# Aligned register loads, earlier scatters of the last tiles and an earlier row table in a routed-expert kernel

## The chip, the cores and the metric

The kernel runs on one core of one Trainium2 chip. The metric is device time in microseconds (us) of one launch. The time before is 1503.49 us, the median of three runs (1494.99 to 1507.39).

## The reference

Two layers act on x, 4 sequences of 512 tokens with 512 features (2048 tokens). Layer 0 is a decayed scan over a context of 1024 tokens with two projections, then a gated feed-forward of width 2048 with Hadamard transforms. Layer 1 is an attention over the same context, then a routed feed-forward: 32 experts, the best 8 for each token. The change concerns that last part alone:

```python
router_logits = x2d @ gate_kernel                      # 2048 tokens x 32 experts
routing_weights = jax.nn.softmax(router_logits, axis=-1)
routing_weights, selected_experts = jax.lax.top_k(routing_weights, TOP_K)
routing_weights = routing_weights / jnp.sum(routing_weights, axis=-1, keepdims=True)
w0 = jax.lax.ragged_dot(sorted_inputs, gate_proj, group_sizes, ...)
w1 = jax.lax.ragged_dot(sorted_inputs, up_proj, group_sizes, ...)
inter = jax.nn.silu(w0) * w1
expert_out = jax.lax.ragged_dot(inter, down_proj, group_sizes, ...)
output = jnp.einsum('BKE,BK->BE', per_token, routing_weights)
```

The output is x plus this sum.

## The kernel before, in words

**Sorting.** The 2048 tokens are 16 tiles of 128 rows. For each tile VectorE computes eight places (POS), one for each chosen expert, and GpSimd writes the tile's rows into the DRAM tensor `rows_by_expert` with eight indirect DMAs (`scatter_rows`, L572 to L578), one for each column of POS. Column w of the last three tiles (13, 14 and 15) counts up the semaphore `s_add[w]`; all other scatters count up `s_ids`. The order written out at the end is: tile 13 all eight columns, tile 14 columns 0 to 3, tile 15 columns 0 to 3, and then columns 4 to 7, each for tile 14 and tile 15 (L589 to L594). SyncE meanwhile writes, one after another, a block of padding rows behind each expert's rows (`pad_expert`).

**Tables.** Each expert's rows are padded to whole tiles of 128, so that up to 159 expert tiles (NTILE) are worked off. How many tiles an expert has is known only at run time. PE and VectorE therefore compute (L1555 to L1593) a table TAB of 5 rows of 168 int32 entries (TABLE), in one partition of the buffer EX: row 0 the expert of a tile, row 1 how many pads and expert weights must have landed before it (`due`), row 2 where its weights lie, row 3 its first row in `rows_by_expert`, row 4 the tile where its expert begins. When all is written, `s_tab` is set to 1.

**Where TAB lies.** EX is cut up by a helper `ex(n)` that hands out n float32 entries after the last ones: TCMP 84 entries, CE 1, CI 2, CH 1, TWK 672, and then TAB. So TAB begins at entry 760 of EX, and its rows follow at distances of 168. In both kernels EX itself begins at byte 207232 of a partition, a multiple of 64.

**The expert loop.** All engines run a loop of 19 rounds (LOOPS) of 8 tiles (U), and then 7 tiles (REST). At the start of each round every engine loads what it needs from TAB into its registers with one instruction for each table row (TENSOR_LOAD in the profile). The helpers are `load_ints` (the load is L104) and `load_counts` (the load is L112, and then L114 raises each value to a least one):

- PE: row 2, 12 entries from it\*8 (L104).
- VectorE: row 0, 8 entries from it\*8 (L104).
- ScalarE: row 3, 12 entries from it\*8 + 4 (L104), then row 1, 12 entries from it\*8 + 2 (L112).
- GpSimd: row 4, 8 entries from it\*8 (L112).

Per tile PE transposes the gathered rows of tile t+2 (L1964), waits for VectorE's product of tile t, transposes it (L1981, L1982), multiplies tile t+1 by its expert's gate and up weights (L1702 to L1704, 384 columns), waits for the hidden activations of tile t, split into a high part by ScalarE (`hidden_hi`, L842) and a low part by VectorE (`hidden_lo`, L1603), and multiplies them by the down weights (L1702 to L1704, L1992, L1993, 512 columns). ScalarE's round is written as: the two register loads, then for each tile `hidden_hi`, `tile_hi` (L834), the DMA that gathers a later tile (`load_tile`, L856), and `tile_silu` (L838). GpSimd adds each finished tile to the output with an indirect DMA (L605).

**The first tiles.** ScalarE waits for the scatters of the last tiles' column 0 (`s_add[0]`) and gathers tile 0. It then waits for `s_tab`, loads the first six entries of rows 1 and 3 with one register load (L864), gathers tiles 1 to 3, works on tile 0 and gathers tiles 4 and 5. Tile t waits for column t's scatters too.

```python
act.wait_ge(s_add[0], LANDED)
load_tile(0, 0, 0, 16)
act.wait_ge(s_tab, 1)
act.reg_load(entries, TAB[0:1, 1:4:2, 0:LEAD])
...
with act.Fori(0, LOOPS) as it:
    rows, due = rows_at("tile_row", it * U + 4, U + 4), experts_due("tile_due", it * U + 2, U + 4)
```

Of the kernel before, what the change touches and what calls it, by code (L numbers as in the profile page):

```python
# [22 lines left out]
P = 128  # L23
# [15 lines left out]
TABLE = NTILE + 9  # L39
# [86 lines left out]
def build(nc, a_x, a_ctxT, a_ctxr, a_kv, a_mask, a_winT, a_woutT, a_cols, a_rows, a_wug, a_wdT,  # L126
          a_gk, a_exp, a_ident, a_had, a_hadf, a_tri, d_exp, d_kv, d_row, d_down, a_out):
    ctx = ExitStack()
    with ctx:
# [3 lines left out]
        def sem(name):  # L133
            return ctx.enter_context(nc.semaphore(name))
# [152 lines left out]
        TCMP = ex(TABLE // 2, F16)  # L287
        CE = ex(1)
        CI = ex(2, I32)
        CH = ex(1, F16)  # L290
        TWK = ex(4 * TABLE, p=1).rearrange("p (a t) -> p a t", a=4)

        TAB = ex(5 * TABLE, I32, p=1).rearrange("p (a t) -> p a t", a=5)
# [57 lines left out]
        s_tp, s_tq, s_tab = sem("table_product"), sem("table_step"), sem("tables_ready")  # L351
# [11 lines left out]
        def _(sp):  # L363
# [151 lines left out]
            sp.wait_ge(s_tpad, 2)  # L515
            for e in range(2 * WP):
                pad_expert(e, 16 * e)
            sp.wait_ge(s_tab, 1)

            def replace_expert(e, h):  # L520
                wait_apart(sp, s_wl, e * 16, s_spassed)
# [16 lines left out]
        def _(pool):  # L538
# [59 lines left out]
            pool.sem_inc(s_y, V)

# [18 lines left out]
        def _(act):  # L618
# [226 lines left out]
                return load_ints(act, name, TAB[0:1, 3, bass.ds(t, count)], 0, NE * CAP + (SPARES - 1) * P)  # L845

            def experts_due(name, t, count):
                return load_counts(act, name, TAB[0:1, 1, bass.ds(t, count)], 16, 16 * NE)

            def load_tile(u, used, row, pads):  # L850

# [8 lines left out]
            act.wait_ge(s_add[0], LANDED)  # L860
            load_tile(0, 0, 0, 16)
            act.wait_ge(s_tab, 1)
            entries = [act.alloc_register(f"first{i}") for i in range(2 * LEAD)]
            act.reg_load(entries, TAB[0:1, 1:4:2, 0:LEAD])  # L864
            rows = [act.snap(x, donate=True, min_val=0, max_val=NE * CAP + (SPARES - 1) * P) for x in entries[LEAD:]]
            due = [act.alloc_register(f"first_due{i}") for i in range(LEAD)]
            for to, of in zip(due, entries):
                act.reg_alu(to, of, 16, ALU.max)
                act.free_register(of)
            due = [act.snap(x, donate=True, min_val=16, max_val=16 * NE) for x in due]  # L870
            act.wait_ge(s_spare, 16)
# [35 lines left out]
        def _(dve):  # L907
# [651 lines left out]
            v.tensor_scalar(CI[0:NE, 1:2], CI[0:NE, 0:1], 7, None, ALU.logical_shift_right).then_inc(s_tq, 1)  # L1559
            dve.wait_ge(s_tq, 2)  # L1560
            v.tensor_copy(CH[0:NE, 0:1], CI[0:NE, 1:2]).then_inc(s_tq, 1)
            dve.wait_ge(s_tp, 2)
            v.tensor_copy(CE[0:NE, 0:1], PS[0:NE, 1, 0:1]).then_inc(s_tq, 1)
            v.tensor_copy(CH[0:NE, 1:2], PS[0:NE, 1, 0:1]).then_inc(s_tq, 1)
            dve.wait_ge(s_tq, 4)
            v.tensor_scalar(TCMP[0:NE, :], TROW[0:NE, :], CE[0:NE, 0:1], None, ALU.is_ge).then_inc(s_tq, 1)
            dve.wait_ge(s_tp, 3)
            erow, start = PS[0:1, 2, 0:TABLE], PS[0:1, 2, TABLE:2 * TABLE]
            trow = TROW[0:1, :]
            v.tensor_scalar(TAB[:, 0, :], erow, NE - 1.0, None, ALU.min).then_inc(s_tq, 1)  # L1570
            v.tensor_scalar(TAB[:, 1, :], erow, NE - 1.0, 1.0, ALU.min, ALU.add).then_inc(s_tq, 1)
            v.scalar_tensor_tensor(TWK[:, 0, :], erow, float(LIST), trow, ALU.mult, ALU.add).then_inc(s_tq, 1)
            v.scalar_tensor_tensor(TWK[:, 2, :], trow, 1.0 - SPARES, start, ALU.add, ALU.subtract).then_inc(s_tq, 1)
            v.tensor_scalar(TCUM[:, :], PS[0:1, 2, 2 * TABLE:2 * TABLE + NE], 1.0, None, ALU.add).then_inc(s_tq, 1)
            dve.wait_ge(s_tq, 10)
            v.tensor_scalar(TAB[:, 2, :], TAB[:, 0, :], WP - 1, None, ALU.bitwise_and).then_inc(s_tq, 1)
            v.tensor_scalar(TAB[:, 1, :], TAB[:, 1, :], 16, None, ALU.mult).then_inc(s_tq, 1)
            v.tensor_tensor(TWK[:, 1, :], TWK[:, 0, :], start, ALU.subtract).then_inc(s_tq, 1)

            v.scalar_tensor_tensor(TWK[:, 3, :], erow, float(NE), TWK[:, 2, :], ALU.is_ge, ALU.mult).then_inc(s_tq, 1)  # L1580
            dve.wait_ge(s_tq, 15)
            v.tensor_scalar(TAB[:, 2, :], TAB[:, 2, :], E16, None, ALU.mult).then_inc(s_tq, 1)
# [3 lines left out]
            dve.wait_ge(s_tq, 19)
            v.tensor_scalar(TODD[:, :], TODD[:, :], SPARES - 1, None, ALU.bitwise_and).then_inc(s_tq, 1)
            dve.wait_ge(s_tq, 20)
            v.tensor_tensor(TAB[:, 3, :], TAB[:, 3, :], TODD[:, :], ALU.add).then_inc(s_tq, 1)
# [53 lines left out]
        def _(pe):  # L1643
# [310 lines left out]
            pe.wait_ge(s_tq, 6)  # L1954
# [135 lines left out]
```

## Time and profile before

| | us |
|---|---|
| median of three runs | 1503.49 |
| the three runs | 1494.99, 1507.39, 1503.49 |
| the profiled execution, its own time | 1494.65 |
| its span, first to last instruction | 1492.9 |

The profile is one execution. Engines are PE (matmul), PEld (weight load), DVE (VectorE), ACT (ScalarE), POOL (GpSimd) and SP (SyncE). A q behind an engine (ACTq) marks what its instruction queue does itself, as a register load, without the engine's arithmetic being busy. "x19" counts instructions, "idle before <-" names what ended an engine's wait. In the chain of waits "issue" is time in which the engine waited for nothing that the profile shows.

### The profile page before, as it was taken

The page shows a single profiled execution, that of the slowest core. Times are in us where ns is not written, and L with a number is a line of the kernel's source. Part 1 is how long each engine was busy: PE and PEld are TensorE (multiplying, and loading weights), DVE is VectorE, ACT ScalarE, POOL GpSimd, SP SyncE. Part 2 cuts the span into 40 slices and gives each one's busy share as a digit, 9 for nine tenths or more (in the row PEclk, how much of TensorE's full clock was granted, in tenths as well). Part 3 has the DMA queues.
Part 4 walks back from the last instruction along what each step waited for, and adds up shares of the span by engine and source line. Part 5 has one row for each costly group of instructions (what it writes and reads, how often), then busy time and mean ns, then how long its engine had stood idle before and what let it go on. Part 6 is the DMA issues. An engine that isn't in the chain of part 4 may idle for free.

```text
span 1492.9 us, 27045 instructions
## 1 busy us (share of the span) xinstructions
PE 1384.7 (93%) x7525; PEld 756.2 (51%) x7526; DVE 1021.5 (68%) x2467; ACT 505.9 (34%) x916; POOL 383.3 (26%) x313
## 2 busy tenths in 40 slices
PE   4899999999999999999998499999999998998997
PEld 2344444444444444455554265555665655565554
DVE  7879857976985656788877366666665655565664
ACT  0445543434444434422222123223332322232222
POOL 1000000000000000036667433433433444333343
PEclk9899999999999999999999699999999999999998
DMA  9976776766667787648769888888988888888785
GB/s 370 379 267 211 254 250 219 248 196 211 232 221 222 236 280 261 232 167 303 284 235 353 270 218 222 199 225 228 243 223 217 217 207 211 175 194 204 130 146 84
DMA packets 132696, 345.04 MB, mean 231 GB/s; under 512 B 15008, under 2 KB 19616, under 8 KB 125728
## 3 DMA queue, kind: packets, MB, share of 16 engines
q1 hardware_dynamic: 73488, 206.72, 41.1%
q0 software_dynamic: 34640, 85.74, 26.0%
q10 hardware_dynamic: 24512, 51.89, 11.0%
q8 instruction: 27, 0.44, 0.1%
q14 instruction: 29, 0.24, 0.1%
HBM read 192.68 MB, written 151.62 MB: 231 GB/s over the span
## 4 chain that ended last, share of the span: by engine, by line
PE 66%; DVE 13%; DMA 6%; ACTq 5%; issue 4%; ACT 3%; SPq 1%; DVEq 0%; POOLq 0%
PE PS L1702 17%; PE PS L1704 17%; PE PS L1703 17%; PE PS L1964 4%; ACTq L112 4%; DMA CST<-in_kv 2%; PE PS L1993 2%; PE PS L1992 2%; DMA split_experts<-HT 2%; DMA rows_by_expert<-X 1%; ACTq L104 1%; PE PS L1981 1%; PE PS L1982 1%; DVE HT L1148 1%; DMA X<-in_x 1%
## 5 line engine op out<-in xcount | busy, mean ns | idle before, releaser
L605 POOL DMA_INDIRECT out<-BIG,EX x159 | 247.1, 1554 | 396.6 <-issue 208.6
L1702 PE MATMUL PS<-BIG 128*128 (+1 forms) x795 | 269.5, 339 | 43.9 <-DVE BIG L1603 42.3
L1704 PE MATMUL PS<-BIG 128*128 (+1 forms) x795 | 269.5, 339 | 0.0
L1703 PE MATMUL PS<-BIG 128*128 (+1 forms) x795 | 269.4, 339 | 0.0
L1702 PE MATMUL PS<-HT,BIG 128*128 128x512 f16 (+1 forms) x512 | 194.1, 379 | 3.2 <-DVE HT L1132 1.4
L1703 PE MATMUL PS<-HT,BIG 128*128 128x512 f16 (+1 forms) x512 | 194.1, 379 | 0.0
L1704 PE MATMUL PS<-HT,BIG 128*128 128x512 f16 (+1 forms) x512 | 194.0, 379 | 0.0
L842 ACT ACTIVATE BIG<-PS 128x256 f16<-128x256 f32 x159 | 60.9, 383 | 298.4 <-PE PS L1982 209.1
L577 POOL DMA_INDIRECT rows_by_expert<-HT,POS x128 | 124.8, 975 | 99.5 <-DVE POS L1422 64.4
L1703 PE MATMUL PS<-BIG,EX 128*128 128x512 f16 (+1 forms) x376 | 143.2, 381 | 0.0
L1704 PE MATMUL PS<-BIG,EX 128*128 128x512 f16 (+1 forms) x376 | 143.2, 381 | 0.0
L1702 PE MATMUL PS<-BIG,EX 128*128 128x512 f16 (+1 forms) x376 | 143.0, 380 | 0.0
L1603 DVE TENSOR_TENSOR BIG<-PS,BIG 128x256 f16<-128x256 f32 x159 | 67.4, 424 | 94.8 <-ACT BIG L842 93.7
L1607 DVE SCALAR_TENSOR_TENSOR BIG<-PS,BIG 128x192 f32<-128x192 f32 x159 | 56.6, 356 | 100.3 <-ACT BIG L838 100.3
L1702 PEld LDWEIGHTS PS<-BIG 128*128 128x128 f16 x795 | 78.1, 98 | 92.4 <-issue 52.9
L1598 DVE SCALAR_TENSOR_TENSOR BIG<-PS,BIG 128x512 f16<-128x512 f32 x159 | 109.9, 691 | 15.8 <-ACT BIG L834 5.7
L1616 DVE TENSOR_SCALAR BIG<-PS,BIG 128x512 f32<-128x512 f32 x159 | 119.3, 751 | 0.0
L668 ACT ACTIVATE HT<-HT 128x1280 f16<-128x1280 f32 x64 | 81.2, 1268 | 95.2 <-DMA split_experts<-HT 93.9
L1964 PE MATMUL PS<-ident,BIG 128*128 128x128 f32 x636 | 98.7, 279 | 11.8 <-DMA BIG<-rows_by_expert 10.1
L569 POOL MEMSET HT<- 128x105 f32 x1 | 0.2, 185 | 422.6 <-DMA split_experts<-HT 422.6
L1704 PEld LDWEIGHTS PS<-BIG 128*128 128x128 f16 x795 | 78.3, 98 | 58.7 <-issue 1.4
L838 ACT ACTIVATE BIG<-PS 128x192 f32<-128x192 f32 x159 | 52.5, 330 | 153.4 <-PE PS L1704 153.4
(264 smaller groups left out, 2254.5 us busy)
## 6 DMA issues: line engine op xcount, KB each, us to landing
BIG<-rows_by_expert ACTq DMA_DIRECT2D x159, 280.0 KB, 4.8
HT<-in_experts SPq DMA_DIRECT2D x64, 640.0 KB, 4.7
BIG<-split_experts SPq DMA_DIRECT2D x32, 1152.0 KB, 8.4
split_experts<-HT SPq DMA_DIRECT2D x96, 320.0 KB, 2.4
CST<-in_kv SPq DMA_DIRECT2D x64, 256.0 KB, 4.8
split_context<-RT SPq DMA_DIRECT2D x64, 256.0 KB, 4.5
BIG<-split_context SPq DMA_DIRECT2D x7, 2048.0 KB, 11.4
rows_by_expert<-X SPq DMA_DIRECT2D x32, 280.0 KB, 7.8
```

What stands on the lines that cost most here:

```text
L112: eng.reg_load(loaded, table)
L577: pool.indirect_dma_start(d_row, bass.IndirectOffsetOnAxis(ap=POS[:, t % ZN, c:c + 1], axis=0), ZR[:, t % ZN, :], None).then_inc(s_ids[t % ...
L605: pool.indirect_dma_start(a_out, bass.IndirectOffsetOnAxis(ap=IDY[:, u % V:u % V + 1], axis=0), yt[u % V], None, compute_op=ALU.add).then_ ...
L668: act.activation(eoh, est[h], ACT.Copy, scale=E_S).then_inc(s_eh, 1)
L842: act.activation(eah[p], PS[:, 4, 0:2 * P], ACT.Copy).then_inc(s_ah2, 1)
L1598: v.scalar_tensor_tensor(xl[p], PS[:, p, :].rearrange("p (k n) -> p k n", n=P), H_S, xh[p], ALU.mult, ALU.subtract).then_inc(s_xl, 1)
L1603: v.tensor_tensor(eal[p], PS[:, 4, 0:2 * P], eah[p], ALU.subtract).then_inc(s_al2, 1)
L1616: v.tensor_scalar(yt[u % V], PS[:, 5 + u % 2, :], xg[u][:, bass.ds(e + D, 1)], None, ALU.mult).then_inc(s_y, 1)
L1702: mm(out, lh, rh, start=first, stop=False)
L1703: mm(out, lh, rl, start=False, stop=False)
L1704: return mm(out, ll, rh, start=False, stop=last_group)
L1964: last = nc.tensor.transpose(PS[:, u % 2, k * P:(k + 1) * P], xg[u][:, k * P:(k + 1) * P], ident[:, :])
```

## The change

1. **Due table shifted.** Row 1 is stored two entries later (DUE = 2), and ScalarE reads it at t + DUE. The load at each round's start now begins at entry it\*8 + 4 of the row; before it was it\*8 + 2.
2. **First load split.** The first register load (two rows of six) becomes two loads of eight entries, each from entry 0 of its row.
3. **Scatter order.** Tile 13 scatters five columns first and its columns 5 to 7 later, in turn with those of tiles 14 and 15.
4. **Table order.** The row numbers (row 3) and dues (row 1) are computed first and `s_tab` is set to 1 behind them; the rest follows and sets it to 2. A further small matmul gives part of the row number. ScalarE waits for 1, the others for 2.
5. **Space.** CH grows from one to two entries of EX for that matmul. What comes after it in EX is handed out one entry later: TAB begins at entry 761.

```diff
+DUE = 2
...
-        CH = ex(1, F16)
+        CH = ex(2, F16)
...
-            sp.wait_ge(s_tab, 1)
+            sp.wait_ge(s_tab, 2)
...
-            scatter_rows(NT - 3)
+            scatter_rows(NT - 3, range(5))
             for t in range(NT - 2, NT):
                 scatter_rows(t, range(4))
             for w in range(4, TOPK):
-                for t in range(NT - 2, NT):
+                for t in range(NT - 3 + (w == 4), NT):
                     scatter_rows(t, (w,))
...
-                return load_counts(act, name, TAB[0:1, 1, bass.ds(t, count)], 16, 16 * NE)
+                return load_counts(act, name, TAB[0:1, 1, bass.ds(t + DUE, count)], 16, 16 * NE)
...
-            entries = [act.alloc_register(f"first{i}") for i in range(2 * LEAD)]
-            act.reg_load(entries, TAB[0:1, 1:4:2, 0:LEAD])
+            entries = [act.alloc_register(f"first{i}") for i in range(2 * U)]
+            act.reg_load(entries[0:U], TAB[0:1, 1, 0:U])
+            act.reg_load(entries[U:], TAB[0:1, 3, 0:U])
...
+            v.tensor_scalar(CH[0:NE, 2:3], CI[0:NE, 1:2], -1.0, float(LIST), ALU.mult, ALU.add).then_inc(s_tq, 1)
...
+            v.tensor_tensor(TWK[:, 1, :], place, trow, ALU.add).then_inc(s_tq, 1)
+            v.tensor_scalar(TAB[:, 1, DUE:TABLE], erow[:, 0:TABLE - DUE], NE - 1.0, 1.0, ALU.min, ALU.add).then_inc(s_tq, 1)
...
+            v.scalar_tensor_tensor(TAB[:, 3, :], TODD[:, :], float(P), TAB[:, 3, :], ALU.mult, ALU.add).then_inc(s_tq, 1)
+            dve.wait_ge(s_tq, 14)
+            dve.sem_inc(s_tab, 1)
...
+            mm(PS[0:1, 6, 0:TABLE], CH[0:NE, 2:3], TCMP[0:NE, :], start=True, stop=True)
...
-            pe.wait_ge(s_tab, 1)
+            pe.wait_ge(s_tab, 2)
```

GpSimd's queue at the last three tiles, before (x8 and the like count equal instructions, "waits" names a semaphore; `places_ready` is set once for each tile):

```order
45 L577 DMA rows_by_expert<-HT,POS 70144x560 [waits places_ready]
46 L577 DMA rows_by_expert<-HT,POS 70144x560 x7
47 L577 DMA rows_by_expert<-HT,POS 70144x560 [waits places_ready]
48 L577 DMA rows_by_expert<-HT,POS 70144x560 x3
49 L577 DMA rows_by_expert<-HT,POS 70144x560 [waits places_ready]
50 L577 DMA rows_by_expert<-HT,POS 70144x560 x3
51 L577 DMA rows_by_expert<-HT,POS 70144x560 [waits places_ready] x8
```

The same place, now:

```order
45 L578 DMA rows_by_expert<-HT,POS 70144x560 [waits places_ready]
46 L578 DMA rows_by_expert<-HT,POS 70144x560 x4
47 L578 DMA rows_by_expert<-HT,POS 70144x560 [waits places_ready]
48 L578 DMA rows_by_expert<-HT,POS 70144x560 x3
49 L578 DMA rows_by_expert<-HT,POS 70144x560 [waits places_ready]
50 L578 DMA rows_by_expert<-HT,POS 70144x560 x3
51 L578 DMA rows_by_expert<-HT,POS 70144x560 [waits places_ready] x11
```

Tile 15's first scatter (row 49) stands behind nine scatters of the three tiles where it stood behind twelve; three move to the end. The number of scatters is the same.

ScalarE's queue from the first gather to the loop's first `hidden_hi`, before:

```order
374 L856 DMA BIG<-rows_by_expert 128x560 [waits rows_sorted5,last_rows_then_tile_added0,rows_sorted4,expert_padded,rows_sorted3,rows_sorted2]
375 L864 TENSOR_LOAD EX [waits tables_ready]
376 L868 ISA
377 L856 ISA [waits expert_padded,last_rows_then_tile_added1,spare_rows_stored]
378 L856 DMA BIG<-rows_by_expert 128x560
...
392 L104 TENSOR_LOAD EX
393 L112 ISA
394 L112 TENSOR_LOAD EX
395 L114 ISA x2
396 L841 REGISTER_ALU
397 L842 ACTIVATE BIG<-PS 128x256 [waits hidden_transposed]
```

And now:

```order
374 L857 DMA BIG<-rows_by_expert 128x560 [waits rows_sorted5,last_rows_then_tile_added0,rows_sorted4,expert_padded,rows_sorted3,rows_sorted2]
375 L865 TENSOR_LOAD EX [waits rows_then_all_tables_ready]
376 L866 TENSOR_LOAD EX
377 L870 ISA
378 L857 ISA [waits expert_padded,last_rows_then_tile_added1,spare_rows_stored]
379 L857 DMA BIG<-rows_by_expert 128x560
...
393 L105 TENSOR_LOAD EX
394 L113 ISA
395 L113 TENSOR_LOAD EX
396 L115 ISA x2
397 L842 REGISTER_ALU
398 L843 ACTIVATE BIG<-PS 128x256 [waits hidden_transposed]
```

One register load was added ahead of the loop. In the loop the instructions and their order are the same; only the addresses of the loads differ.

## Rows read from the trace of the kernel before

**Rows 1.** The page: busy time, and the chain that ended last by engine.

```profile
PE 1384.7 (93%) x7525; PEld 756.2 (51%) x7526; DVE 1021.5 (68%) x2467; ACT 505.9 (34%) x916; POOL 383.3 (26%) x313
...
PE 66%; DVE 13%; DMA 6%; ACTq 5%; issue 4%; ACT 3%; SPq 1%; DVEq 0%; POOLq 0%
```

**Rows 2.** The chain of waits, whole execution, by line.

```profile
by line: PE PS L1702 17.0%; PE PS L1704 16.7%; PE PS L1703 16.7%; issue 4.3%; PE PS L1964 4.1%; ACTq L112 3.9%; DMA CST<-in_kv 2.3%; PE PS L1993 2.1%; PE PS L1992 2.1%; DMA split_experts<-HT 1.7%; DMA rows_by_expert<-X 1.3%; ACTq L104 1.1%;
```

**Rows 3.** The waits from 850 to 1485 us: total us, times, longest.

```profile
POOL out L605 <- DVE BIG L1616: 135.5, 46, 11.5
...
ACT BIG L842 <- issue: 83.5, 18, 6.4
...
PE PS L1702 <- DVE BIG L1603: 42.3, 20, 3.7
```

**Rows 4.** The chain of waits at one round's start: start us, us, what.

```profile
972.44 0.04 ACT BIG L838
...
972.83 0.78 ACTq L104
...
973.72 2.64 ACTq L112
...
976.68 0.39 ACT BIG L842
...
977.66 0.39 PE PS L1702
```

**Rows 5.** Register loads by line, whole execution: count, ns min/median/max, first and last start.

```profile
L112 POOLq TENSOR_LOAD <-EX x20: 572/582/2302, 829.3 to 1460.1; - x20
L112 ACTq TENSOR_LOAD <-EX x20: 1876/2807/4792, 845.7 to 1457.9; - x20
...
L104 PEldq TENSOR_LOAD <-EX x20: 847/956/2377, 839.8 to 1457.0; - x20
L104 DVEq TENSOR_LOAD <-EX x20: 601/631/1707, 843.5 to 1458.8; - x20
L104 ACTq TENSOR_LOAD <-EX x20: 296/800/1555, 844.0 to 1457.6; - x20
...
L864 ACTq TENSOR_LOAD <-EX x1: 3490/3490/3490, 831.5 to 831.5; - x1
```

**Rows 6.** PE's own register load at the round's start of rows 4.

```profile
L104 PEldq TENSOR_LOAD <-EX x1: 937/937/937, 972.2 to 972.2; - x1
```

**Rows 7.** PE's timeline at three rounds' starts: start us, us.

```profile
946.44 0.39 PE L1702 MATMUL PS<-BIG 128*128 x1 [2.53 <-DVE BIG L1603]
...
973.33 0.65 PE L1964 MATMUL PS<-ident,BIG 128*128 128x128 f32 x4
...
977.66 0.39 PE L1702 MATMUL PS<-BIG 128*128 x1 [1.52 <-DVE BIG L1603]
...
1136.03 0.45 PE L1702 MATMUL PS<-BIG 128*128 x1 [3.08 <-DVE BIG L1603]
```

**Rows 8.** Windows: us, busy PE PEld DVE ACT POOL, granted clock, DMA share, GB/s.

```profile
1134.00:1138.00 4.00, 1.97 (x6) 0.90 (x7) 1.51 (x4) 1.17 (x3) 0.00 (x0) 0.78 0.62 138
1138.00:1142.00 4.00, 4.00 (x22) 2.75 (x21) 2.05 (x5) 1.20 (x3) 3.11 (x2) 0.80 0.51 72
```

**Rows 9.** Timeline at the first expert tiles.

```profile
823.02 0.17 DVE L1422 TENSOR_SCALAR POS<-M 128x8 int32<-128x8 f32 x1
...
827.72 0.96 POOL L577 DMA_INDIRECT rows_by_expert<-HT,POS  x1 [0.30 <-issue]
...
828.66 0.24 DVE L1591 TENSOR_SCALAR EX<-EX 1x168 int32<-1x168 int32 x1
...
831.09 6.21 ACTq L856 DMA_DIRECT2D BIG<-rows_by_expert  x4
...
835.03 1.11 PE L1964 MATMUL PS<-ident,BIG 128*128 128x128 f32 x4 [10.06 <-DMA BIG<-rows_by_expert]
...
849.06 0.38 ACT L842 ACTIVATE BIG<-PS 128x256 f16<-128x256 f32 x1 [5.77 <-DMA rows_by_expert<-X]
```

More of the change, by code:

```diff
@@ L350, in build @@
         s_pd, s_spare, s_pad, s_res = (sem(n) for n in ("pads_step", "spare_rows_stored", "expert_padded", "residual_stored"))
-        s_tp, s_tq, s_tab = sem("table_product"), sem("table_step"), sem("tables_ready")
+        s_tp, s_tq, s_tab = sem("table_product"), sem("table_step"), sem("rows_then_all_tables_ready")
         s_wl = sem("expert_landed")
@@ L592, in _ @@
             for w in range(4, TOPK):
-                for t in range(NT - 2, NT):
+                for t in range(NT - 3 + (w == 4), NT):
                     scatter_rows(t, (w,))
-            pool.wait_ge(s_tab, 1)
+            pool.wait_ge(s_tab, 2)
             pool.wait_ge(s_res, 16 * B)
@@ L862, in _ @@
             act.wait_ge(s_tab, 1)
-            entries = [act.alloc_register(f"first{i}") for i in range(2 * LEAD)]
-            act.reg_load(entries, TAB[0:1, 1:4:2, 0:LEAD])
-            rows = [act.snap(x, donate=True, min_val=0, max_val=NE * CAP + (SPARES - 1) * P) for x in entries[LEAD:]]
-            due = [act.alloc_register(f"first_due{i}") for i in range(LEAD)]
-            for to, of in zip(due, entries):
+            entries = [act.alloc_register(f"first{i}") for i in range(2 * U)]
+            act.reg_load(entries[0:U], TAB[0:1, 1, 0:U])
+            act.reg_load(entries[U:], TAB[0:1, 3, 0:U])
+            rows = [act.snap(x, donate=True, min_val=0, max_val=NE * CAP + (SPARES - 1) * P) for x in entries[U:]]
+            due = [act.alloc_register(f"first_due{i}") for i in range(U - DUE)]
+            for to, of in zip(due, entries[DUE:U]):
                 act.reg_alu(to, of, 16, ALU.max)
+            for of in entries[0:U]:
                 act.free_register(of)
@@ L1564, in _ @@
             v.tensor_copy(CH[0:NE, 1:2], PS[0:NE, 1, 0:1]).then_inc(s_tq, 1)
-            dve.wait_ge(s_tq, 4)
+            dve.wait_ge(s_tq, 5)
             v.tensor_scalar(TCMP[0:NE, :], TROW[0:NE, :], CE[0:NE, 0:1], None, ALU.is_ge).then_inc(s_tq, 1)
             dve.wait_ge(s_tp, 3)
-            erow, start = PS[0:1, 2, 0:TABLE], PS[0:1, 2, TABLE:2 * TABLE]
+            place, erow, start = PS[0:1, 6, 0:TABLE], PS[0:1, 2, 0:TABLE], PS[0:1, 2, TABLE:2 * TABLE]
             trow = TROW[0:1, :]
+            v.tensor_tensor(TWK[:, 1, :], place, trow, ALU.add).then_inc(s_tq, 1)
@@ new lines, in _ @@
+            v.tensor_scalar(TAB[:, 1, DUE:TABLE], erow[:, 0:TABLE - DUE], NE - 1.0, 1.0, ALU.min, ALU.add).then_inc(s_tq, 1)
+            dve.wait_ge(s_tq, 8)
+            v.tensor_scalar(TODD[:, :], TWK[:, 1, :], -float(NE * LIST), 0.0, ALU.add, ALU.max).then_inc(s_tq, 1)
+            v.tensor_scalar(TAB[:, 3, :], TWK[:, 1, :], float(NE * LIST), float(P), ALU.min, ALU.mult).then_inc(s_tq, 1)
+            dve.wait_ge(s_tq, 10)
+            v.tensor_scalar(TODD[:, :], TODD[:, :], SPARES - 1, None, ALU.bitwise_and).then_inc(s_tq, 1)
@@ L1570, in _ @@
+            v.tensor_scalar(TAB[:, 1, DUE:TABLE], TAB[:, 1, DUE:TABLE], 16, None, ALU.mult).then_inc(s_tq, 1)
+            dve.wait_ge(s_tq, 12)
+            v.scalar_tensor_tensor(TAB[:, 3, :], TODD[:, :], float(P), TAB[:, 3, :], ALU.mult, ALU.add).then_inc(s_tq, 1)
+            dve.wait_ge(s_tq, 14)
+            dve.sem_inc(s_tab, 1)
             v.tensor_scalar(TAB[:, 0, :], erow, NE - 1.0, None, ALU.min).then_inc(s_tq, 1)
-            v.tensor_scalar(TAB[:, 1, :], erow, NE - 1.0, 1.0, ALU.min, ALU.add).then_inc(s_tq, 1)
@@ L1572, in _ @@
-            v.scalar_tensor_tensor(TWK[:, 0, :], erow, float(LIST), trow, ALU.mult, ALU.add).then_inc(s_tq, 1)
             v.scalar_tensor_tensor(TWK[:, 2, :], trow, 1.0 - SPARES, start, ALU.add, ALU.subtract).then_inc(s_tq, 1)
             v.tensor_scalar(TCUM[:, :], PS[0:1, 2, 2 * TABLE:2 * TABLE + NE], 1.0, None, ALU.add).then_inc(s_tq, 1)
-            dve.wait_ge(s_tq, 10)
+            dve.wait_ge(s_tq, 15)
             v.tensor_scalar(TAB[:, 2, :], TAB[:, 0, :], WP - 1, None, ALU.bitwise_and).then_inc(s_tq, 1)
-            v.tensor_scalar(TAB[:, 1, :], TAB[:, 1, :], 16, None, ALU.mult).then_inc(s_tq, 1)
@@ L1578, in _ @@
-            v.tensor_tensor(TWK[:, 1, :], TWK[:, 0, :], start, ALU.subtract).then_inc(s_tq, 1)
+            dve.wait_ge(s_tq, 16)
             v.scalar_tensor_tensor(TWK[:, 3, :], erow, float(NE), TWK[:, 2, :], ALU.is_ge, ALU.mult).then_inc(s_tq, 1)
-            dve.wait_ge(s_tq, 15)
+            dve.wait_ge(s_tq, 18)
             v.tensor_scalar(TAB[:, 2, :], TAB[:, 2, :], E16, None, ALU.mult).then_inc(s_tq, 1)
-            v.tensor_scalar(TAB[:, 3, :], TWK[:, 1, :], float(NE * LIST), None, ALU.min).then_inc(s_tq, 1)
@@ L1584, in _ @@
-            v.tensor_scalar(TODD[:, :], TWK[:, 1, :], -float(NE * LIST), 0.0, ALU.add, ALU.max).then_inc(s_tq, 1)
+            dve.wait_ge(s_tq, 19)
             v.tensor_tensor(TAB[:, 4, :], TWK[:, 3, :], start, ALU.add).then_inc(s_tq, 1)
[L1586 to L1589, printed above, removed]
@@ L1590, in _ @@
             dve.wait_ge(s_tq, 21)
-            v.tensor_scalar(TAB[:, 3, :], TAB[:, 3, :], P, None, ALU.mult).then_inc(s_tq, 1)
-            dve.wait_ge(s_tq, 22)
             dve.sem_inc(s_tab, 1)
@@ L1953, in _ @@
             mm(PS[0:NE, 1, 0:1], tri[0:NE, 1, 0:NE], CH[0:NE, 0:1], start=True, stop=True).then_inc(s_tp, 1)
-            pe.wait_ge(s_tq, 6)
+            pe.wait_ge(s_tq, 7)
+            mm(PS[0:1, 6, 0:TABLE], CH[0:NE, 2:3], TCMP[0:NE, :], start=True, stop=True)
             mm(PS[0:1, 2, 0:TABLE], tri[0:NE, 2, 0:1], TCMP[0:NE, :], start=True, stop=True)
```

## The prediction, made before the changed kernel ran

> **What bounds the kernel now.** I read the page first. PE is busy 93% of the span, and it is 66% of the chain that ended last; but 5% of that chain is ACTq, ScalarE's instruction queue, and not its arithmetic [rows 1]. The chain by line says what that is: L112 is 3.9% and L104 1.1%, the two register loads at the start of each round of the expert loop [rows 2]. Next come the waits of the expert stage: ScalarE's `hidden_hi` (L842) stands 18 times behind "issue" for 83.5 us together, and PE's down product (L1702) waits 42.3 us in 20 waits for `hidden_lo` (L1603) [rows 3]. So PE bounds seven tiles of eight, and at each round's first tile ScalarE's register loads do, for 42.3 / 20 = 2.1 us.
>
> The chain at one round's start shows the order. ScalarE's last activation of the old round starts at 972.44, the row load takes 0.78 us from 972.83, the due load 2.64 us from 973.72, `hidden_hi` starts at 976.68, and PE goes on at 977.66 [rows 4], after a wait of 1.52 us [rows 7]. Whatever the two loads gain or lose beyond these 1.52 us of wait goes straight into the time; a loss goes in whole.
>
> **What a register load costs.** Both ScalarE loads have 12 entries, yet the median is 0.800 us for L104 and 2.807 us for L112 [rows 5]. They differ in where they start. Counted in EX, whose own start is a multiple of 64 bytes, L104 begins at 760 + 3\*168 + 4 = 1268 plus 8 per round, a multiple of four entries (16 bytes). L112 begins at 760 + 168 + 2 = 930 plus 8 per round, two past a multiple. The other loads of the loop all begin at multiples of four and are cheap: PE 12 entries 0.956, VectorE 8 entries 0.631, GpSimd 8 entries 0.582 [rows 5]. From 8 to 12 entries costs about 0.2 us, 0.05 for each entry. The cheapest load, one entry, takes 0.296 [rows 5], so an unaligned load pays (2.807 - 0.296) / 11 = 0.23 for each further entry. I read this as: entries are fetched four at a time where the address is a multiple of 16 bytes, and one at a time elsewhere.
>
> The Trainium skill (page "Runtime: NRT & Kernel Launch", section "Instruction fetch mechanics") puts such loads at about 200 ns for each register, in bulk too. The due load agrees with it (2.807 / 12 = 0.23 us); the row load does not (0.800 / 12 = 0.07).
>
> **The change, part by part.**
>
> *Loads of the loop.* Shifting the due table by two entries would make L112 begin at a multiple of four, if TAB still did. It doesn't: CH took one more entry of EX, so TAB begins at 761. The due load now begins at 761 + 168 + 4 = 933, and the row load at 761 + 504 + 4 = 1269, both one past a multiple of four, and so do the loads of PE, VectorE and GpSimd. By my reading nothing gets faster, and every load of the loop gets the unaligned price.
> - ScalarE: the due load stays at 2.8 (bounds 0.8, if it did become aligned, and 2.8). The row load goes from 0.80 to 2.81, 2.0 more by the medians. By the whole chain, with the starts at which DMA traffic slows the loads, it is (3.9% - 1.1%) x 1492.9 / 18 = 2.3 [rows 2]. I take 2.2. Nothing hides it, as PE waits already. 19 x 2.2 = 42 us (38 to 44).
> - PE: its load began at 972.2 and took 0.94 us [rows 6], hidden behind the last products of the old round: the transposes start at 973.33 [rows 7]. With 2.0 more it ends at 975.2, so PE stands still 1.8 us there. From the transposes to the end of the up products is 977.66 - 1.52 - 973.33 = 2.8 us, so PE is ready at 978.0. ScalarE's side is ready at 977.66 + 2.0 = 979.7. PE's load is covered by ScalarE's; if it weren't there, PE's alone would cost 1.8 - 1.52 = 0.3 each. I count 0.
> - VectorE and GpSimd: 8 entries one by one are 0.296 + 7 x 0.23 = 1.9, 1.3 more. VectorE's next work waits for the same late `hidden_hi`. GpSimd waits 135.5 us in this stretch for VectorE's results [rows 3], over five times 19 x 1.3 = 25, which is what it would cost without that cover. I count 0.
>
> *Scatters.* A scatter takes 0.96 us with 0.30 ahead of it, 1.27 from one to the next [rows 9]. Tile 15's column 0 starts at 827.72; ScalarE gathers tile 0 at 831.09, and PE sits idle 10.06 us until it has landed at 835.03 [rows 9]. Three scatters fewer are ahead of it: 827.72 - 3.8 = 823.9, which is still after tile 15's places (823.02 + 0.17 [rows 9]). So all of it counts: -3.8 us (bounds -3.8 and 0, if something else held tile 0 up). The columns 5 to 7 of tile 13 come later, but the last scatter ends when it did, before 849.06, when the first round's `hidden_hi` starts.
>
> *Tables earlier.* The table's last instruction ends at 828.9 [rows 9], and ScalarE asks for it only behind its gather at 831.09. With the gather at 827.3 that would become a wait of 1.6 us. Of the sixteen instructions ahead of the signal seven are left; nine at 0.24 us or more are 2.2, so rows and dues are there by about 826.8, even with one more matmul and one more VectorE instruction ahead. This part earns nothing by itself, it keeps the 3.8 whole. The others wait for the second signal, with about as many instructions ahead as before; PE's load starts only at 839.8 [rows 5].
>
> *First load split.* 3.49 us [rows 5] becomes two loads of eight: 2 x 1.9 unaligned, with 0.75 for a first use (1.555 against 0.800 [rows 5]) 4.5; aligned it would be 1.3 or more. Tile 1's gather still moves from 835 to about 832, as it starts 3.8 earlier, and PE wants it behind tile 0's products. 0 either way.
>
> **The sum.** On the profiled execution: 1494.65 - 3.8 + 42 = 1532.9 us. That execution lies 8.8 below the median of the runs; the mean of all four times is 1500.1. I start from that: 1500.1 - 3.8 + 42 = **1538 us**.
>
> **The rivals.**
>
> *A, the clock falls too.* The granted clock was 0.78 and 0.80 in the 8 us around a wait of 3.08 us [rows 7, 8]: 4 x (0.22 + 0.20) = 1.7 us lost. After a wait of 2.53 the first product still takes 0.39, as after 1.52 [rows 7]. I expect 3.5 us of idle at a typical start, but in two pieces of 1.8 and 1.7 with matmuls between. Should the clock fall each time, 19 x 1.7 = 32 is added: 1570. For it: the slow starts would now pass 3 us often. Against: each piece is under 2.53.
>
> *B, the start of a load is not what costs.* The first load L864 begins both its rows at multiples of four (928 and 1264) and still takes 3.49; L112 on ScalarE also differs from L104 in being the second of two, into registers that don't all follow one another. Then the loop stays as it is, and only the scatters count: 1500.1 - 3.8 = 1496. This rival is not slower than before. It decides if the row load stays at 0.8 although it begins at 1269. Against it: GpSimd's L112, the same helper, takes 0.582 for 8 entries from a multiple of four, and L864 is a load in two rows, which may never go by fours. The rule of the Trainium skill's page named above, one price for each register whatever the address, would leave the loop unchanged too.
>
> *C, it does what it is written to do.* If alignment counted from something other than the address in EX, so that row and due loads were both at 0.8, ScalarE would be 2.0 earlier at each start, 19 x 2.0 = 38 of PE's 42.3 us: 1500.1 - 3.8 - 38 = 1458. Against: the row load's cheap start and the due load's dear one are both told by the address in EX, and no start one past a multiple is in the trace.
>
> **How the numbers follow.** My forecast has 0.70, A 0.10, B 0.14, C 0.05, and 0.01 is left for others. Forecast and A together run from 1494.65 - 3.8 + 19 x 1.86 (the two loads of [rows 4], 2.64 - 0.78) = 1526, less 10 for the runs' scatter (they lie 12 apart), to A at 1570. That range leaves out B and C, 0.19. A measurement of this kernel can tell about 1% from no change. Slower by over 1% (above 1518.5): forecast and A, 0.80. Within 1%: most of B, 0.13. Faster: C and a little of B, 0.07.
>
> **What would show it.** Right: ScalarE's and PE's L104 (one line lower now) at about 2.8 and 2.9 us, VectorE's and GpSimd's loads at 1.9, the due load unchanged; PE's down product waiting about as often, and a new wait ahead of the transposes; tile 0's gather issued near 827.3. Wrong: a row load at 0.8 (B), or a due load at 0.8 (C). If the loads are all dear and the time has hardly moved, my claim that PE waits for ScalarE at each start is what failed.

## The result, and the profile after

The changed kernel is slower: 1532.80 us (median of four runs, 1527.74 to 1538.02) against 1500.33 us (four runs, 1494.99 to 1507.39). The ratio is 1.0214, with a 95% interval from 1.0155 to 1.0272: clearly slower, though whether by 2% the interval leaves open. The profiled executions are 1527.74 and 1494.65 us, 33.1 apart. The forecast was 1538 us, slower by over 1% with a chance of 0.80. One run of the experiments below, 1493.02 us of a kernel whose other three lie between 1467.10 and 1470.19, was in a slower state of the chip and is left out of its median and ratio.

The page of the changed kernel, to set beside [rows 1]:

```profile
span 1525.9 us, 27048 instructions
...
PE 1391.2 (91%) x7526; PEld 756.1 (50%) x7527; DVE 1020.4 (67%) x2466; ACT 505.6 (33%) x916; POOL 383.3 (25%) x313
...
PE 72%; DVE 9%; ACTq 8%; DMA 4%; issue 3%; ACT 2%; SPq 1%; POOLq 0%; DVEq 0%
```

ACTq has gone from 5% of the chain to 8%: the chain now holds two dear register loads at each round's start. The register loads by line show it directly (lines are one lower down than before; columns as in [rows 5]):

```profile
L105 PEldq TENSOR_LOAD <-EX x20: 1760/3166/7152, 838.7 to 1489.7; - x20
L105 DVEq TENSOR_LOAD <-EX x20: 1851/2060/5251, 840.6 to 1491.5; - x20
L105 ACTq TENSOR_LOAD <-EX x20: 294/2819/5529, 841.1 to 1490.3; - x20
...
L113 POOLq TENSOR_LOAD <-EX x20: 1621/2608/4137, 830.4 to 1492.8; - x20
L113 ACTq TENSOR_LOAD <-EX x20: 1866/2800/4467, 846.7 to 1490.6; - x20
...
L865 ACTq TENSOR_LOAD <-EX x1: 3995/3995/3995, 827.1 to 827.1; - x1
...
L866 ACTq TENSOR_LOAD <-EX x1: 3743/3743/3743, 831.1 to 831.1; - x1
```

ScalarE's row load, 0.800 us before, has a median of 2.819; the due load, which the edit was about, stays at 2.800. PE's went from 0.956 to 3.166, VectorE's from 0.631 to 2.060, GpSimd's from 0.582 to 2.608. The forecast had 2.8, 2.9, 1.9 and 1.9, so PE's and above all GpSimd's median came out dearer. Where that ends up is in the waits of the expert stage (from 845 us on, columns as in [rows 3]):

```profile
POOL out L606 <- DVE BIG L1622: 147.6, 47, 11.7
DVE BIG L1609 <- ACT BIG L843: 132.2, 139, 9.0
ACT BIG L843 <- issue: 129.2, 19, 9.7
...
PE PS L1971 <- issue: 47.8, 20, 6.4
...
PE PS L1708 <- DVE BIG L1609: 24.4, 18, 3.3
```

Before there was one wait of PE at each round's start, 42.3 us in all. Now there are two: one ahead of the transposes (L1971), behind PE's own register load, 47.8 us, and one ahead of the down product (L1708), 24.4 us. Together that is 72.2. A single round's start in the chain of waits (to set beside [rows 4]) and in PE's timeline:

```profile
979.08 0.04 ACT BIG L839
...
979.47 2.60 ACTq L105
...
982.19 2.62 ACTq L113
...
985.13 0.39 ACT BIG L843
```

```profile
981.93 0.65 PE L1971 MATMUL PS<-ident,BIG 128*128 128x128 f32 x4 [1.81 <-issue]
...
986.11 0.39 PE L1708 MATMUL PS<-BIG 128*128 x1 [1.36 <-DVE BIG L1609]
```

The forecast had 1.8 us for the first wait and 1.7 for the second; they are 1.81 and 1.36 here.

### The profile page after: what moved, and what is told of

Read it like the earlier page. It is cut to its first block, busy times and chain, and to the rows that moved or that the text cites. A ratio compares the mean times of both kernels' runs of the same rounds, so it can differ in the third digit from the quotient of the medians.

```text
span 1525.9 us, 27048 instructions
## 1 busy us (share of the span) xinstructions
PE 1391.2 (91%) x7526; PEld 756.1 (50%) x7527; DVE 1020.4 (67%) x2466; ACT 505.6 (33%) x916; POOL 383.3 (25%) x313
## 4 chain that ended last, share of the span: by engine, by line
PE 72%; DVE 9%; ACTq 8%; DMA 4%; issue 3%; ACT 2%; SPq 1%; POOLq 0%; DVEq 0%
PE PS L1708 19%; PE PS L1710 19%; PE PS L1709 19%; PE PS L1971 4%; ACTq L113 4%; ACTq L105 4%; PE PS L2000 2%; PE PS L1999 2%; DMA split_experts<-HT 2%; DMA BIG<-in_wdT 1%; PE PS L1662 1%; PE PS L1988 1%; PE PS L1989 1%; DMA CST<-in_kv 1%; PE PS L1885 1%
## 5 line engine op out<-in xcount | busy, mean ns | idle before, releaser
L1708 PE MATMUL PS<-BIG 128*128 (+1 forms) x795 | 273.4, 344 | 26.1 <-DVE BIG L1609 24.4
L1709 PE MATMUL PS<-BIG 128*128 (+1 forms) x795 | 273.3, 344 | 0.0
L1710 PE MATMUL PS<-BIG 128*128 (+1 forms) x795 | 273.0, 343 | 0.0
L1708 PE MATMUL PS<-HT,BIG 128*128 128x512 f16 (+1 forms) x512 | 194.1, 379 | 3.4 <-DVE HT L1135 1.4
L1609 DVE TENSOR_TENSOR BIG<-PS,BIG 128x256 f16<-128x256 f32 x159 | 67.5, 424 | 133.6 <-ACT BIG L843 132.2
L1971 PE MATMUL PS<-ident,BIG 128*128 128x128 f32 x636 | 98.7, 279 | 55.2 <-issue 47.8
L1708 PE MATMUL PS<-BIG,EX 128*128 128x512 f16 (+1 forms) x376 | 143.0, 380 | 0.1
L1971 PEld LDWEIGHTS PS<-ident,BIG 128*128 128x128 f32 x636 | 79.1, 143 | 92.5 <-issue 57.9
L1708 PEld LDWEIGHTS PS<-BIG 128*128 128x128 f16 x795 | 79.1, 100 | 76.8 <-issue 38.3
```

Of the source, the lines that this page charges most:

```text
L1609: v.tensor_tensor(eal[p], PS[:, 4, 0:2 * P], eah[p], ALU.subtract).then_inc(s_al2, 1)
L1708: mm(out, lh, rh, start=first, stop=False)
L1709: mm(out, lh, rl, start=False, stop=False)
L1710: return mm(out, ll, rh, start=False, stop=last_group)
L1971: last = nc.tensor.transpose(PS[:, u % 2, k * P:(k + 1) * P], xg[u][:, k * P:(k + 1) * P], ident[:, :])
```

## The experiments

All times are medians. The kernel before was run beside each, and ratios are to it; they are worked out from all runs of both kernels, so they differ a little from the quotient of two medians. The kernel before took 1501.99 us beside the first four kernels below (`a_tab764`, `b_tab761`, `b_tab762`, `a_tab764_due0`) and 1504.73 us beside `c_before_due2`, `c_old_scatters`, `c_pe_off` and `c_dve_pool_off`. The other three ran on a chip where it took 1525.24 us, so only their ratios compare with the rest.

**TAB moved to a multiple of four.** One line ahead of TAB in the changed kernel:

```diff
+        ex(3)
         TAB = ex(5 * TABLE, I32, p=1).rearrange("p (a t) -> p a t", a=5)
```

> The changed kernel with TAB moved three entries on, to entry 764 of EX, a multiple of four; nothing else differs. Address theory (entries are fetched by fours where the load begins at a multiple of 16 bytes): all loads of the loop are cheap, ScalarE's row and due load both 0.80 us, PE's 0.96, VectorE's and GpSimd's about 0.6; ScalarE's idle time at a round's start falls from 6.6 us to about 2.7, PE waits at hardly any start, and the time is 1500.3 - 42 = 1458 us or, with 4 us for the start of the expert stage, 1454. Theory that the kind of load or its registers set the price: the loads stay as in the changed kernel, 2.8 us, and the time stays at 1533.

Measured: 1449.78 us, ratio 0.9666 (0.9628 to 0.9704). That is below both times expected, 1458 and 1454. Three unused entries turn the slower kernel into one that beats both. Its page, loads and waits (from 843 us on):

```profile
PE 1378.0 (95%) x7526; PEld 753.9 (52%) x7527; DVE 1022.3 (71%) x2466; ACT 506.2 (35%) x916; POOL 384.0 (27%) x313
```

```profile
L105 PEldq TENSOR_LOAD <-EX x20: 846/905/2560, 835.2 to 1408.1; - x20
L105 DVEq TENSOR_LOAD <-EX x20: 602/623/1683, 839.1 to 1410.0; - x20
L105 ACTq TENSOR_LOAD <-EX x20: 299/800/2582, 840.5 to 1408.7; - x20
...
L113 ACTq TENSOR_LOAD <-EX x20: 566/791/1562, 843.2 to 1409.0; - x20
```

```profile
ACT BIG L844 <- issue: 15.8, 4, 5.9
...
PE PS L1709 <- DVE BIG L1610: 6.1, 5, 3.3
PE PS L1972 <- issue: 0.8, 2, 0.5
```

The due load is at 0.791 us in the same registers and in the same place, second of two, as when it took 2.8. PE waits 6.9 us where it waited 72.2, which is 65.3 of the 81.9 us between the two spans. Another 13.2 are PE's busy time, 1391.2 against 1378.0, for the same matmuls: the mean granted clock is 0.975 in the one execution and 0.982 in the other. Against the kernel before, 1384.7, it is 6.7 us, which the expected times did not count.

**The kernel before with TAB one entry on.** One line again:

```diff
+        ex(1)
         TAB = ex(5 * TABLE, I32, p=1).rearrange("p (a t) -> p a t", a=5)
```

> The kernel before with one unused entry ahead of TAB, so that it begins at entry 761; nothing else differs. Address theory: L104 on ScalarE goes from 0.80 to 2.8 us and on PE from 0.96 to 3.2, and the time goes to that of the changed kernel or a little less, as the other edits don't act: 1500.3 + 32 = 1532 us (1525 to 1540). Any theory in which the shifted due table, the split first load, the scatter order or the table order costs the time: 1500 us.

Measured: 1533.62 us, ratio 1.0216 (1.0177 to 1.0255), the time of the changed kernel, whose ratio is 1.0214. One unused float gives the whole loss, within these intervals; the shift, the split first load, the scatter order and the table order have no part in it that shows. The first load, in two rows of six, shows the address too: 3.490 us at entry 760 [rows 5], and here

```profile
L865 ACTq TENSOR_LOAD <-EX x1: 6137/6137/6137, 833.9 to 833.9; - x1
```

Each is a single load; at entry 762 it took 6.175 us.

**The kernel before with TAB two entries on.** The same line with `ex(2)`.

> The kernel before with two unused entries ahead of TAB (entry 762). The due load then begins at a multiple of four (932) and all the others two past one: the prices of ScalarE's two loads change places, row 2.8 and due 0.8 us, with the same instructions and registers. Address theory: just that; the sum on ScalarE stays 3.6 us and the time stays within 1% of 1500, with a wait of about 1.8 us ahead of PE's transposes that moves PE's wait from the one place to the other. Theory that the second of two loads or scattered registers are dear: the due load stays at 2.8 us and the row load at 0.8 us.

Measured: 1509.15 us, ratio 1.0052 (1.0023 to 1.0081).

```profile
L104 ACTq TENSOR_LOAD <-EX x20: 298/2840/4758, 846.1 to 1475.0; - x20
L112 ACTq TENSOR_LOAD <-EX x20: 567/806/2047, 850.3 to 1475.3; - x20
```

```profile
PE PS L1965 <- issue: 47.5, 20, 5.1
...
PE PS L1703 <- DVE BIG L1604: 2.6, 4, 1.1
```

The prices changed places, 2.840 and 0.806 us, with instructions, registers and order the same. That rules out rival B in each of its forms: the kind of load, its place as the second of two, its registers, and one price whatever the address. The time is 0.5% up, as PE's own load is now the later side: 47.5 us of waits ahead of the transposes in place of 42.3 ahead of the down product. Together with the changed kernel it also shows that two entries past a multiple of four (2.840) are as dear as one past (2.819).

**The shift undone, with TAB at 764.**

```diff
-DUE = 2
+DUE = 0
```

> The changed kernel with TAB at entry 764 and the due table not shifted (DUE = 0), so that only the due load begins two past a multiple of four. Address theory: the due load 2.8 us, all others cheap, as in the kernel before; the time is that of before less what the start of the expert stage gains, 1496 us (1492 to 1500), and the difference to the kernel with TAB at 764 and the shift is what the shift is worth, 38 to 42 us.

Measured: 1500.10 us, ratio 0.9995 (0.9974 to 1.0016). The time is just above what was expected (1492 to 1500), and the shift is worth more than the 38 to 42 us expected: 0.9995 - 0.9666 = 0.033, 49 us. PE waited 42.5 us behind L1610 and was busy 1391.6, against 6.1 and 1378.0. So one dear load on ScalarE costs 36 us of wait and 14 of longer busy time. That this is the clock shows in all runs: the mean granted clock is 0.971 to 0.977 in the ten of this kernel and 0.982 to 0.984 in the four of the kernel with all loads aligned.

**Only the due shift, in the kernel before.** TAB at 760, the old table and scatter orders, CH with one entry; the shift and the split first load as in the diff above.

> The kernel before with the due table shifted by two entries and the first register load split, and nothing else: TAB stays at entry 760, CH at one entry, table order and scatter order are the old ones. Address theory: all loads of the loop cheap, and nearly the whole gain of the kernel with TAB at 764: 1450 us plus what the earlier scatters are worth, 1450 to 1454 us. Rival: the new table order or the further matmul carry part of it: 1460 us or more.

Measured: 1449.41 us, ratio 0.9638 (0.9597 to 0.9680). All of the gain is in the shift, with the split first load that goes with it. Table order and scatter order add nothing that shows.

**The old scatter order, with TAB at 764.**

```diff
-            scatter_rows(NT - 3, range(5))
+            scatter_rows(NT - 3)
...
-                for t in range(NT - 3 + (w == 4), NT):
+                for t in range(NT - 2, NT):
```

> The changed kernel with TAB at entry 764 and the old order of the last scatters (tile 13 all eight columns first). My theory of the start: ScalarE's first gather is issued 3.8 us later (near 831), and as nothing else sets the start of the expert stage now that the loads are cheap, the time is 3.8 us more than with the new order (1449.8), 1453.6 us. Rival: the first gather isn't what the first rounds wait for, and the time stays at 1450 (within 1.5).

Measured: 1449.54 us, ratio 0.9639 (0.9608 to 0.9671), against 1449.78 with the new order. As the two had been run at different times on different chips, and their traces hinted at 1 us, I ran the pair again side by side.

> The changed kernel with TAB at entry 764 once more, in five rounds and beside the same kernel with the old order of the scatters, since their first comparison went over two jobs: 1449.8 us again. In the traces of the first pair the third tile's high part starts 29.4 us behind PE's first table matmul with the new order and 30.4 us with the old one, so I expect 1 us between the two; by the step of my forecast it would be 3.8.

> The same with the old order of the last scatters. If the first gather's 3.8 us reached the end, 1453.6 us; if most of it is lost again in the first tiles, as the first pair of traces suggests, 1450 to 1451 us.

Measured: 1478.32 us, ratio 0.9689 (0.9657 to 0.9721), with the new order, 1476.92 us, ratio 0.9683 (0.9650 to 0.9715), with the old one. The old order is not slower, twice. That is the rival of the first text, not my 3.8 us. The second pair says less about the start of the expert stage, though: in its two traces ScalarE's first activation there waited 9.78 and 7.75 us for something that the profile doesn't name, so the gather was not what held it. The timelines of the first pair show where the 3.8 go. New order:

```profile
823.59 0.18 PE L1960 MATMUL PS<-EX,tri 32*32 32x1 f16 x1 [0.76 <-DVE EX L1566]
...
827.31 5.44 ACTq L858 DMA_DIRECT2D BIG<-rows_by_expert  x4
...
844.74 0.39 ACT L844 ACTIVATE BIG<-PS 128x256 f16<-128x256 f32 x1 [5.90 <-issue]
...
853.03 0.38 ACT L844 ACTIVATE BIG<-PS 128x256 f16<-128x256 f32 x1 [1.40 <-PE PS L1990]
```

Old order:

```profile
825.65 0.18 PE L1960 MATMUL PS<-EX,tri 32*32 32x1 f16 x1 [0.76 <-DVE EX L1566]
...
832.99 6.20 ACTq L858 DMA_DIRECT2D BIG<-rows_by_expert  x4
...
849.45 0.38 ACT L844 ACTIVATE BIG<-PS 128x256 f16<-128x256 f32 x1 [4.31 <-issue]
...
856.06 0.38 ACT L844 ACTIVATE BIG<-PS 128x256 f16<-128x256 f32 x1 [1.40 <-PE PS L1990]
```

Counted from PE's table matmul (L1960), the first gather is 3.7 us behind with the new order and 7.3 with the old, 3.6 apart, as forecast. The first high part is 21.2 and 23.8 behind, 2.6 apart, and the third tile's 29.4 and 30.4, 1.0 apart. The traces show where 2.6 of the 3.6 us go. The first round's two register loads on ScalarE took 2.58 and 1.23 us with the new order, 1.98 and 0.79 with the old: 1.0. Then PE works on the first tile and the next transposes (columns as in [rows 8]; new order first):

```profile
845.72:849.63 3.91, 3.91 (x14) 2.42 (x15) 2.03 (x6) 0.73 (x3) 0.00 (x0) 0.56 0.41 137
...
850.43:852.50 2.07, 2.07 (x14) 1.44 (x14) 1.69 (x5) 0.31 (x2) 0.00 (x0) 1.00 0.62 182
```

With the new order these matmuls follow a wait of 3.32 us and the granted clock is 0.56, near 1.2 GHz; with the old one the wait is 1.73 us and the clock 1.00, 2.4 GHz. That makes up the other 1.6. These are two executions, and neither cause was tried by itself. Where the last 1.0 us goes is open.

**Only PE's load off the multiple of four, TAB at 764.**

```diff
-                return load_ints(pe, name, TAB[0:1, 2, bass.ds(t, count)], 0, (WP - 1) * E16)
+                return load_ints(pe, name, TAB[0:1, 2, bass.ds(t + 1, count)], 0, (WP - 1) * E16)
...
-            v.tensor_scalar(TAB[:, 2, :], TAB[:, 0, :], WP - 1, None, ALU.bitwise_and).then_inc(s_tq, 1)
+            v.tensor_scalar(TAB[:, 2, 1:TABLE], TAB[:, 0, 0:TABLE - 1], WP - 1, None, ALU.bitwise_and).then_inc(s_tq, 1)
...
```

> The changed kernel with TAB at entry 764, but the row of weight places stored one entry later and read there, so that only PE's register load begins one past a multiple of four. Theory that PE's sequencer does the load itself and can't issue behind it: L105 on PE 3.0 us or more, a wait of 1.8 to 2.4 us ahead of the transposes at each of 19 starts, and 1450 + 34 to 46 = 1484 to 1496 us. Rival: PE's load is covered by queued matmuls, 1450 us.

Measured: 1503.78 us, ratio 0.9995 (0.9966 to 1.0024). The aligned kernel run beside it, the one with the old scatter order, is at 0.9639, so PE's dear load costs 54 us. That is above the 34 to 46 expected.

```profile
L105 PEldq TENSOR_LOAD <-EX x20: 1781/3118/7813, 838.7 to 1475.4; - x20
```

```profile
PE PS L1972 <- issue: 45.0, 19, 4.1
```

PE's queue can't hide its own dear load. The waits, 45.0 / 19 = 2.4 each, are the upper end of what was expected; the rest is PE's busy time again. The profiled execution overstates it: it was the slowest of ten, 1513.53 us, with 1401.2 us busy against 1378.0. If the waits are alike in the median run, about 10 of the 54 us are left for the longer busy time (an estimate).

**Only VectorE's and GpSimd's loads off, TAB at 764.** The same kind of edit on rows 0 and 4.

> The changed kernel with TAB at entry 764, but the rows that VectorE and GpSimd load stored one entry later and read there, so that only these two loads begin one past a multiple of four. My theory, by which both are covered: both loads go from 0.6 to about 2 us and the time stays at 1450 (within 5). Rival: with ScalarE no longer late, VectorE's 1.3 us more at each start come ahead of the low part of the hidden activations and PE waits for them: up to 19 x 1.3 = 25, 1475 us.

Measured: 1467.42 us (three runs), ratio 0.9762 (0.9711 to 0.9814), so 0.9762 - 0.9639 = 0.012 or 18 us more than with these loads aligned. I had expected none.

```profile
L105 DVEq TENSOR_LOAD <-EX x20: 1853/2253/5198, 839.9 to 1434.0; - x20
```

```profile
DVE BIG L1610 <- issue: 23.1, 9, 5.1
...
PE PS L1709 <- DVE BIG L1610: 21.0, 20, 4.0
```

The rival's 1475 comes nearer than my 1450: once ScalarE is on time, VectorE's low part waits behind VectorE's own load ("issue", 23.1 us), and PE behind that. Nothing in these waits stands behind GpSimd's load, but the two loads were not moved one at a time. In the changed kernel VectorE's load is hidden: its low part (L1609) stands behind ScalarE's high part there, 132.2 us in 139 waits, and not behind a load.

**Plain stores in place of indirect adds.** Some loads take 4 us and more. In the trace of before three of the four longest due loads (4.792, 4.727 and 3.977 us) lay beside 2.8 to 3.5 us of GpSimd's indirect DMAs, so I suspected these. The kernel here, with TAB at 761, stores half of each finished tile in rows behind the output and leaves out the sum over a token's experts.

```diff
-                pool.indirect_dma_start(a_out, bass.IndirectOffsetOnAxis(ap=IDY[:, u % V:u % V + 1], axis=0), yt[u % V], None,
-                                        compute_op=ALU.add).then_inc(s_add[u % V], 16)
+                pool.dma_start(a_out[NTOK + 64 * (u % V):NTOK + 64 * (u % V) + 64, :], yt[u % V][0:64, :]).then_inc(s_add[u % V], 16)
```

> The changed kernel (TAB at 761, all loads dear), but GpSimd stores half of each finished tile with a plain DMA into rows behind the output instead of adding the whole tile to the output with an indirect DMA; the sum over a token's experts is thus left out. Theory that register loads are slowed while GpSimd writes the descriptors of an indirect DMA: ScalarE's loads in the loop no longer spread from 2.6 to 4.5 us but stay at 2.6, ScalarE's idle time at a start falls from 6.6 to about 5.7 us, and the time falls by 15 to 20 us, to 1515. Rival, that other DMA traffic (weights, gathers) slows them: the spread stays, and the time stays within 5 us of 1533.

Measured: 1550.93 us, ratio 1.0184 (1.0135 to 1.0232), against 1.0214 for the changed kernel: 0.3% or 5 us less, with intervals that overlap, where 15 to 20 us less would have borne out the suspicion. The spread stayed:

```profile
L105 ACTq TENSOR_LOAD <-EX x20: 497/2762/4147, 871.2 to 1514.7; - x20
...
L113 ACTq TENSOR_LOAD <-EX x20: 1129/2898/4492, 874.7 to 1515.3; - x20
```

So the indirect adds aren't what stretches most of these loads. The other DMA traffic is the likelier cause. In the two traces of before and of the changed kernel seven full due loads lay beside a DMA share of 0.29 or less, and all took 2.58 to 2.62 us; every full one of 3.0 us or more lay beside a share of 0.56 or more. But many that took 2.6 us lay beside a busy DMA too, and no run tried the gathers, the weight loads or other engines' own register loads by themselves, so it stays open.

## Why the prediction was right, point by point

- **The reading of the load prices held.** Cheap at a multiple of 16 bytes and dear elsewhere: shown by the swap (2.840 and 0.806 us) and by the two kernels that differ by one and three unused entries. Four at a time there and one at a time elsewhere is a reading of the prices that the load behind the loop supports: it has seven entries, and aligned they take PE 1.072 us, longer than its 0.956 for twelve, and GpSimd 1.042 against 0.582 for eight, as one four and three single entries would; unaligned, GpSimd's seven take 1.621, 0.23 each. One surmise beside it was wrong: a load in two rows isn't exempt, it takes 3.490 us at 760 and 6.137 at 761. The Trainium skill's 200 ns for each register ("Runtime: NRT & Kernel Launch", "Instruction fetch mechanics") comes near for unaligned loads alone; at 12 entries in 0.8 us the measurement decides for 0.07. The same page of the Trainium skill (section "The ~15µs preamble/postamble breakdown") says of its loads that they come from HBM, where the ones here come from the on-chip buffer EX.
- **ScalarE's term, 42 us, was too large.** From the first high part to the end the span has 1492.9 - 849.06 = 643.8 us before and 1525.9 - 850.02 = 675.9 after, 32.0 more over 18 further full starts: 1.8 each and not 2.2. ScalarE's idle time grew by 119.5 / 18 - 83.5 / 18 = 2.0. At these starts the row load went from a mean of 0.94 us to 3.04, 2.1 more, and the due load from 3.19 to 3.09, 0.1 less. The term that was mis-sized is the 2.3: it took the difference between the due and the row load of before, slow moments included, for the growth of the row load. What becomes of the last 0.2 us of each start, which "a loss goes in whole" had in the time, is not found. And not all of the 32.0 is waiting: PE was busy 592.2 us in this stretch before and 600.5 after, 8.3 more, so its idle time grew by 23.7.
- **PE's load is covered by ScalarE's, and counted 0: right.** PE's first wait (47.8 us) fills time that ScalarE's later side needs anyway; its second (24.4) is what is left of the old one. By itself PE's load costs 54 us in the aligned kernel. The 19 x 0.3 = 5.7 us that it was to cost in place of ScalarE's came out as 0.5%, 7 to 8 us, with TAB at 762.
- **VectorE and GpSimd, counted 0: right for this kernel,** where VectorE's low part waits for ScalarE's high part and no wait of PE or VectorE stands behind these loads, though they are worth 18 us where ScalarE is on time.
- **The scatters, -3.8 us: wrong.** The timeline of the changed kernel shows the gather at 826.72 and not 831.09, the first step as forecast. The step that failed is "so all of it counts". Two things undo it. In the changed kernel the register loads on ScalarE's way to the first high part ran long: the two first ones took 3.995 + 3.743 = 7.7 us, not 4.5, ahead of tile 1's gather, and the first round's row load took 5.529 us, where it had taken 1.555. The timeline shows the gather, and the chain of waits (the second fence) the loads:

```profile
826.72 10.01 ACTq L857 DMA_DIRECT2D BIG<-rows_by_expert  x4
...
830.05 1.11 PE L1971 MATMUL PS<-ident,BIG 128*128 128x128 f32 x4 [5.70 <-DMA BIG<-rows_by_expert]
...
850.02 0.38 ACT L843 ACTIVATE BIG<-PS 128x256 f16<-128x256 f32 x1 [9.71 <-issue]
```

```profile
831.13 3.74 ACTq L866
...
841.05 5.53 ACTq L105
...
846.69 2.98 ACTq L113
```

  PE's own first load took 7.152 us and held its next transposes up by 6.42 us, until 846.04; that is not on this chain, as ScalarE's loads end later, at 849.67.
  The first high part starts at 850.02, 1.0 later than in [rows 9] in spite of a gather 4.4 earlier. In the aligned kernel, where these loads are cheap, 2.6 us are left of it at the first tile, 1.0 at the third and none in the times.
- **The tables earlier, counted 0: right.** The kernel with the old table order is as fast, 0.9638 against 0.9666.
- **The sum.** Forecast: -3.8 + 42 = 38 us. Measured on the profiled executions: +1.0 + 32.0 = 33. Two wrong sizes of opposite sign partly cancel, 4.8 us too low at the start of the stage and 10 too high in the loop; that the total is only 5 us off is in part luck.
- **Rival A, the clock.** It fell at some starts, not at each. The windows are two due loads of the changed kernel (columns as in [rows 8]):

```profile
982.20:984.82 2.62, 2.55 (x18) 1.50 (x16) 0.00 (x0) 0.00 (x0) 0.00 (x0) 1.00 0.10 32
...
1149.00:1151.59 2.59, 2.59 (x12) 1.58 (x12) 0.00 (x0) 0.00 (x0) 0.00 (x0) 0.55 1.13 230
```

  The first start had waits of 1.81 and 1.36 us and kept the 2.4 GHz; in the second, behind a wait of 2.07 us, the granted clock is 0.55, near 1.2 GHz. Of the 18 due loads at the full starts behind the first, seven lie beside a granted clock of 0.55 to 0.67 and eleven beside 1.00. PE's busy time grew by 1391.2 - 1384.7 = 6.5 us over the whole execution, against 32 for a fall at every start. Part of the slow matmuls costs nothing here: at the start with the 2.07 us they run while ScalarE is still loading, and the down product at 1153.14 then starts without its second wait. That 2.53 us was safe [rows 7] was no bound, then: 2.07 wasn't.
- **Rivals B and C fell by the changed kernel itself:** its row load, at 2.819 us, is not at the 0.8 of B, and its due load, at 2.800, not at the 0.8 of C. The swap rules B out once more.

## What to carry to other kernels

Load tables into registers from addresses that are multiples of 16 bytes, and look at where the allocator puts the table itself, not only at the offsets within it: here one float handed out ahead of it cost 2% and the intended alignment is worth 3.3 to 3.6%. When an engine's instruction queue shows up in the chain of waits, read the register loads by line and engine; here the same 12 entries took 0.8 or 2.8 us. An earlier first transfer is worth only what is left of it some tiles later, so price it there.

## What the runs showed of the hardware that I had not expected

- The cost of a dear load is more than its wait. With one on ScalarE PE was busy 1391.6 us for the matmuls that take 1378.0 without, 14 us on top of 36 of waits; with one on PE it was 1401.2, in an execution 9.7 us above the median. The granted clock fell behind the idle time at some of the starts.
- A load's count matters beside its address. Seven aligned entries took PE 1.072 us and twelve 0.956, its shortest 0.847.
- Unaligned loads were stretched by more microseconds than aligned ones, though not by a larger factor: over the loop ScalarE's loads of twelve took 0.8 us and at most 2.6 aligned, 2.8 and up to 5.5 unaligned. At the start of the stage eight entries took 3.7 to 4.0 us, against 0.8 to 2.2 aligned. GpSimd's indirect adds explain little of it at most, and what does was not tried.
